# Attention over a context in four head pairs: maxima two blocks further ahead, a second buffer for the row sums, the outputs' scaling inside the last pair, and keys loaded early

## The reference

```python
ln = layer_norm(latents); xn = layer_norm(x)          # 512 and 8192 rows of 512
q = (ln @ Wq)                                         # 8 heads of 64, scaled by 64 ** -0.5
k_x, v_x = rope(xn @ Wk), xn @ Wv                     # rope turns halves of 32 within each head
k = concat([k_x, ln @ Wk]); v = concat([v_x, ln @ Wv])   # 8704 keys per head
out = softmax(q @ k.T) @ v                            # per head
x = x + out @ Wo
```

## Time and profile before

| | us |
|---|---|
| median of 3 runs (2338.95 to 2342.64) | 2342.53 |
| the profiled execution's own time | 2343.25 |
| its span | 2341.4 |
| context stage, first unit of maxima to last value product | 83.0 to 466.6 |
| attention, first scores to the next stage's first matmul | 485.3 to 1127.2 |
| TensorE busy in the span | 2171.3 |
| VectorE busy | 1659.6 |
| ScalarE busy | 1100.9 |
| GpSimd busy | 976.2 |

### The profile page before, as it was taken

The page is one execution under the profiler, slowest core; times in us unless marked ns, Lnnn a source line. Parts: engine busy times, 40 slices in busy tenths (PEclk is TensorE's granted clock), DMA queues, the critical chain, the costliest instruction groups (busy, mean ns, idle before and its releaser), DMA issues. The chain is left out here.

```text
span 2341.4 us, 38336 instructions
## 1 busy us (share of the span) xinstructions
PE 2171.3 (93%) x12632; PEld 1100.2 (47%) x12735; DVE 1659.6 (71%) x2398; ACT 1100.9 (47%) x1718; POOL 976.2 (42%) x651
## 2 busy tenths in 40 slices
PE   6899999979999899899699999999999999999858
PEld 2444444423223233233365664757565575757433
DVE  6677777569889889879575756666675756666672
ACT  4122222234444445456364655656464655656343
POOL 0243434469889699788220402122220302222040
PEclk9999999989999999999899999999999999999979
DMA  3345454343322323332323333342323333342330
GB/s 116 132 143 179 140 171 149 101 148 94 87 75 82 127 78 90 117 89 73 119 73 109 97 119 92 127 118 91 114 94 115 93 126 100 119 125 73 94 108 18
DMA packets 159717, 252.60 MB, mean 108 GB/s; under 512 B 11382, under 2 KB 63862, under 8 KB 159606
## 3 DMA queue, kind: packets, MB, share of 16 engines
q1 hardware_dynamic: 159606, 250.96, 33.7%
HBM read 212.00 MB, written 36.70 MB: 106 GB/s over the span
## 5 line engine op out<-in xcount | busy, mean ns | idle before, releaser
L817 POOL TENSOR_TENSOR h_lo<-h_lo,probs 128x896 f32<-128x896 f32 (+1 forms) x272 | 544.6, 2002 | 57.5 <-ACT probs L929 37.2
L63 PE MATMUL l_mm<-l_xt_hi,wt_hi 128*128 128x256 f16 (+3 forms) x1568 | 416.0, 277 | 5.2 <-DVE l_xt_lo L1259 2.8
L1218 POOL TENSOR_TENSOR l_rstd<-l_var_eps,neg_half 128x1 f32<-128x1 f32 x68 | 65.6, 965 | 844.9 <-DVE l_var_eps L1270 844.9
L65 PE MATMUL l_mm<-l_xt_hi,wt_lo 128*128 128x256 f16 (+3 forms) x1568 | 415.2, 276 | 1.4 <-issue 0.7
L64 PE MATMUL l_mm<-l_xt_lo,wt_hi 128*128 128x256 bf16 (+3 forms) x1560 | 412.8, 276 | 0.0
L929 ACT ACTIVATE probs<-sc 128x1024 f32<-128x1024 f32 x272 | 274.5, 1023 | 291.5 <-PE sc L977 239.0
L874 DVE TENSOR_TENSOR h_lo<-h_lo,probs 128x128 f32<-128x128 f32 (+1 forms) x272 | 295.6, 1087 | 24.4 <-ACT probs L929 23.5
L832 DVE TENSOR_REDUCE pmax<-mx 128x1024 f32 x204 | 249.0, 1220 | 41.8 <-PE mx L964 33.1
L988 PE MATMUL pv<-probs,vb 128*64 128x512 f32 x1088 | 268.4, 615 | 0.0
L976 PE MATMUL sc<-q_hi,ka 128*128 128x512 f16 x544 | 212.5, 391 | 13.2 <-DMA kh<-keys 5.9
L65 PE MATMUL l_tok<-wt_hi,h_lo 128*128 128x512 f16 x576 | 218.3, 379 | 1.7
(11 more groups left out here) (268 smaller groups left out, 3651.4 us busy)
## 6 DMA issues: line engine op xcount, KB each, us to landing
stage<-in_L_attn_Wf SPq DMA_DIRECT2D x64, 1024.0 KB, 5.2
keys<-wt_hi SPq DMA_DIRECT2D x136, 128.0 KB
ka<-keys SPq DMA_DIRECT2D x68, 256.0 KB, 3.3
vb<-values SPq DMA_DIRECT2D x68, 256.0 KB, 5.6
stage<-in_ctx SPq DMA_DIRECT2D x16, 1024.0 KB, 9.7
values<-wt_lo SPq DMA_DIRECT2D x16, 1024.0 KB
stage<-in_L_ffn_f SPq DMA_DIRECT2D x16, 1024.0 KB, 5.4
kh<-keys SPq DMA_DIRECT2D x68, 128.0 KB, 5.3
```

Source lines behind the costliest of these rows:

```text
L63: pe.matmul(out, lh, rh, start=first, stop=False, **kw)
L65: return pe.matmul(out, ll, rh, start=False, stop=last, **kw)
L817: g.tensor_tensor(sums[:, mine], sums[:, mine], probs[j][:, mine], ALU.add)\
```

## The change

- **Maxima two blocks further ahead.** While pair p works on block b, the maxima are those of the next pair's block b + 2 (max_block); in the last two blocks they are blocks 0 and 1 of the pair after next. For pair 1 these two come from the context stage, as four late units each in blocks 1 and 2, from a second set of km copies. Block 15's units of pair 0 also become late units, inside block 15. Odd pairs keep blocks 0 and 1 in two more columns of pmax, and the blocks are taken in another order (max_memory).
- **Pairs without a break.** pair_max and rows_of_maxima come before the last block or two of a pair, the first two score steps of the next pair inside its last block, row_sums behind the next pair's first block. There are two tiles sums.
- **Outputs.** ScalarE copies pv behind the next pair's first exponential and side in its second block, for each pair into its own place. The reciprocals of pairs 0 to 2 are taken in pair 3 behind blocks 1, 4 and 7; pair 3's reads side and pv directly.
- **Keys early.** ka and kh for blocks 0 and 1 of pair 0 are loaded in context block 15, in the place of res; the constant rows of kh are set at the program's start.

```diff
+MAX_COLS = KB + 2
+EARLIER_OUT = (1, 4, 7)
...
+        def earlier_units(b):
+            return TT * b + (2 * TT if not isinstance(b, int) or b >= 3 else TT if b == 2 else 0)
+        def late_pair(i, u):
+            b = 2 * i + u
+            if isinstance(b, int) and b in (1, 2):
+                return b - 1, 1
+            return (b, 0) if isinstance(b, int) and b == CTX_BLOCKS - 1 else None
...
@@ context_phase, SyncE, body
-                        sp.wait_ge(mx_ready, TT * b)
+                        sp.wait_ge(mx_ready, earlier_units(b))
...
+                    if late_pair(i, u) and late_pair(i, u)[1]:
+                        sp.wait_ge(mx_ready, earlier_units(b) + TT)
+                        sp.sem_inc(passed, 1)
+                        load_km(1 - u, 1 - u, 1)
                     for hl, done in enumerate((k_hi_done, k_lo_done)):
                         sp.wait_ge(done, 4 * b + 4)
...
+                    if not before_end(i, u, 1):
+                        for n in range(2):
+                            sp.wait_ge(stored[n], STORES * (HALF_BLOCKS - 1))
+                            k.load_k(sp, 0, n, n)
...
@@ context_phase, TensorE, body
                     values(i, u, 0)
+                    late_unit(0)
                     if more:
                         transposes(*nxt, 0)
                         transposes(*nxt, 1)
                     values(i, u, 1)
+                    late_unit(1)
...
@@ attention_phase
-        sums = rows(k.h_lo, 8, 4)
+        sums = [rows(k.h_lo, 8, 4), slots(k.wt_lo, 0, 1, F32, 2 * TOK)[:, 0]]
...
+        def max_block(p, b):
+            if isinstance(b, int) and b >= TURN:
+                return p + 2, b - TURN
+            return p + 1, b + 2
...
@@ VectorE
-                for n in range(2):
-                    v.memset(kh[n][HD:HD + 1], M_UNIT).then_inc(consts, 1)
...
+                            if b in EARLIER_OUT:
+                                n = EARLIER_OUT.index(b)
+                                dve.wait_ge(pv_copied, n + 1)
+                                dve.wait_ge(sums_copied, n + 1)
+                                out_scale(n, o_sum[:, n, :], o_raw[:, n, :])
+                            if b - 1 in EARLIER_OUT:
+                                out_low(EARLIER_OUT.index(b - 1))
...
+                        with dve.Fori(FIRST_PIECE + 1, TURN) as b:
+                            block_work(p, b, True)
+                    pair_max(p + 1)
+                    for b in range(TURN, KB):
+                        block_work(p, b, p > 0)
...
+                out_scale(PAIRS - 1, side[:], pv[:])
                 out_low(PAIRS - 1)
@@ ScalarE
+                    for b in range(2):
                         for j in range(SUB):
+                            exponential(p, b, j)
+                            if p and b == 0 and j == 0:
+                                out_copy(p - 1)
+                            if p and b == 1 and j == 1:
+                                sums_copy(p - 1)
...
+                    for j in range(SUB):
+                        exponential(p, KB - 1, j)
+                        if j == 1:
+                            row_maxima(p + 1)
@@ TensorE
                             elif not last:
-                                scores(p, i, u + 1, n) if u == 0 else scores(p, i + 1, 0, n)
+                                scores(p, b + 1, i, n)
+                            elif p + 1 < PAIRS:
+                                if n == 0:
+                                    pe.wait_ge(rows_done, 2 * (p + 2))
+                                scores(p + 1, 0, 0, n)
+                        if isinstance(i, int) and b == 0 and j == 0:
+                            if p:
+                                pe.wait_ge(pv_copied, p)
+                            t_.matmul(pv[:], zero[:], k.q_hi[:, 0, :], start=True, stop=False)
...
                 for p in range(PAIRS):
+                    block_steps(p, 0)
                     if p:
                         row_sums(p - 1)
-                        pe.wait_ge(out_copied, 2 * p)
...
+                    block_steps(p, KB - 2)
                     if p + 1 < PAIRS:
                         rows_of_maxima(p + 1)
+                    block_steps(p, KB - 1)
```

More of the change, by code:

```diff
@@ L40, with km_rows @@
     pass
-KM_ROWS = [(slice(HD * e + 32 * half, HD * e + 32 * half + 32), (slice(32 * e, 32 * e + 32), half))
-           for e in range(2) for half in range(2)]
+def km_rows(pair):
+    return [(slice(HD * e + 32 * half, HD * e + 32 * half + 32), (slice(HD * pair + 32 * e, HD * pair + 32 * e + 32), half))
+            for e in range(2) for half in range(2)]
 def slots(w, first, count, dtype, width):
@@ L360, in context_phase @@
         STORES = 16 * (2 * PAIRS + 1)
+        KM_IN = 16 * len(km_rows(0))
         def over_blocks(eng, body):
-            for u in range(2):
-                body(0, u)
-            with eng.Fori(1, HALF_BLOCKS - 2) as i:
+            for b in range(4):
+                body(b // 2, b % 2)
+            with eng.Fori(2, HALF_BLOCKS - 2) as i:
                 for u in range(2):
@@ L393, in load_tab, with load_km @@
                     sp.dma_start(tab[u][:], tab_v[2 * i + u]).then_inc(tab_in[u], 16)
+                def load_km(slot, u, pair):
+                    for rows_, (part, m) in km_rows(pair):
+                        sp.dma_start(km[slot][rows_, :], kt[u][part, 0, m, :]).then_inc(km_in[slot], 16)
                 def store_keys(i, u, hl, tile):
@@ L675, in body @@
                     values(i, u, 2)
+                    late_unit(2)
                     if more:
@@ L678, in body @@
                     values(i, u, 3)
+                    late_unit(3)
                 over_blocks(pe, body)
-                last = CTX_BLOCKS - 1
-                for j in range(TT):
-                    unit_max(TT + TT * last + j, 1, j, HALF_BLOCKS if j == 0 else None)
 def attention_phase(k):
@@ L720, in attention_phase @@
         side = pb("side", [P, TOK], F32)
-        k_loaded = [sem(f"a_k_loaded{n}") for n in range(2)]
         v_loaded = [sem(f"a_v_loaded{n}") for n in range(2)]
@@ L883, in _ @@
-                    with dve.Fori(0, KB - PIECES + 1 if p else KB) as b:
-                        block_work(b, False)
+                    if p == PAIRS - 1:
+                        for b in range(KB):
+                            if b == FIRST_PIECE + 1:
+                                dve.wait_ge(w_staged, 16 * STAGES * p)
+                            block_work(p, b, b > FIRST_PIECE)
+                            if b in EARLIER_OUT:
[5 more added lines that the diff above has]
+                                out_low(EARLIER_OUT.index(b - 1))
+                        weight_low(p, KB)
+                        continue
@@ L931, in _ @@
-                    with act.Fori(0, KB - PIECES if p else KB) as b:
-                        exponentials(b)
+                            exponential(p, b, j)
[3 more added lines that the diff above has]
+                                sums_copy(p - 1)
+                    if p == PAIRS - 1:
+                        for b in range(2, KB):
+                            if b == FIRST_PIECE:
+                                act.wait_ge(w_staged, 16 * STAGES * p)
+                            for j in range(SUB):
+                                exponential(p, b, j)
+                                if j == 1 and b - 1 in EARLIER_OUT:
+                                    out_high(EARLIER_OUT.index(b - 1))
+                            if b >= FIRST_PIECE:
+                                weight_high(p, b)
+                        continue
@@ L933, in _ @@
+                    with act.Fori(2, FIRST_PIECE if p else KB - 1) as b:
+                        for j in range(SUB):
+                            exponential(p, b, j)
                     if p:
                         act.wait_ge(w_staged, 16 * STAGES * p)
-                        with act.Fori(KB - PIECES, KB) as b:
-                            exponentials(b)
-                            n = b - (KB - PIECES)
-                            a.activation(hi_pieces[:, bass.ds(4 * XWO + PIECES * (p - 1) + n, 1), :],
-                                         staged_pieces[:, bass.ds(n, 1), :], ACT.Copy).then_inc(w_hi, 1)
@@ L940, in _ @@
-                    if p + 1 < PAIRS:
-                        row_maxima(p + 1)
-                    act.wait_ge(sums_ready, p + 1)
-                    if p >= 2:
-                        act.wait_ge(out_scaled, p - 1)
-                    a.activation(o_sum[p % 2], side[:], ACT.Copy).then_inc(out_copied, 1)
-                    a.activation(o_raw[p % 2], pv[:], ACT.Copy).then_inc(out_copied, 1)
+                        with act.Fori(FIRST_PIECE, KB - 1) as b:
+                            for j in range(SUB):
+                                exponential(p, b, j)
+                            weight_high(p, b)
```

307 lines of the change are left out of this document (168 added, 139 removed).

## The result

| | before | after |
|---|---|---|
| median of 20 runs each, us | 2343.19 (2338.41 to 2348.26) | 2337.49 (2332.49 to 2342.62) |
| ratio, 95% interval | | 0.9975 [0.9967, 0.9983] |
| span of the profiled execution | 2341.4 | 2333.8 |
| first scores of the attention | 485.27 | 502.88 |
| next stage's first matmul | 1127.23 | 1120.56 |

The change gains 5.7 us. The forecast was 2318 with a range to 2333, so the sign is right and the time falls outside the range: some 19 us of the gain are missing. They can be followed stretch by stretch.

The account below looks back on a forecast made before the run. TensorE bounds the context stage; in attention three engines run almost level, with the loss at the seams. 22.2 - 6.6 - 36.5 + 0.5 - 5.4 + 1.0 = -24.8 from 2343.25, less 0.7, gave 2318 us; range 2302 to 2333.

Parts of the forecast that it names:

- context stage, to the last store: Context stage: pair 1's late units, waits for copies and bank, lower clock and block 15's units make it 22.2 us later.
- the tail and the store: Behind the context stage: dropping the tail of four maxima gains hardly anything, early key loads may cost the store 0.5; counted 0.
- attention's start: Attention's opening: without two memsets and with keys loaded early, the chain of maxima alone decides; 6.6 us saved.
- seams (36.5): Three seams between attention pairs: 9.4, 14.7 and 10.9 us saved, plus 1.5 in pair 2's last blocks; together 36.5.
- keys behind weights: Two attention seams: block 2's keys queue right behind three weight loads, landing after they are needed; 1.0 us charged.
- reciprocals in pair 3: Last pair: three reciprocals on VectorE behind blocks 1, 4 and 7, mostly covered by four exponential buffers; 0.5 of 14.1 us charged.
- the end: From the last sums to the next stage: one reciprocal left instead of two in a row, 5.4 us saved.
- The seams' 3.7 us: Cost left at each seam: rows 1.48, sums 1.08, pv bank opening 0.2, pv copy 0.7, switching 0.2; 3.7 us.
- Keys wait at the seams: Rival: scores wait for keys at both seams as in the attention's opening, 10.7 us more than charged, 2329; chance 0.13.
- the reciprocals show: Rival: VectorE cannot catch up in pair 3, so the reciprocals cost 13.6 us more, 2332; chance 0.12.
- Slower than before: Rival: stalls leave TensorE at half clock over context blocks 1 and 2, 43 us more, 2362; chance 0.03.
- the seams stay: Rival: the next pair's scores still meet an unfinished row of maxima, so the 36.5 us remain, 2355; chance 0.03.

Follow-up runs that it names:

- own tiles: Changed kernel, with pair 1's context-stage km copies given two tiles of their own and loaded right behind pair 0's in blocks 0 and 1: 2319.17 us, ratio 0.9895.
- late keys: Changed kernel, with pair 0's first keys loaded at the attention's start again, ahead of the values, not in context block 15: 2335.15 us, ratio 0.9969.

## Why the prediction was wrong, step by step

| step of the prediction | forecast, us | measured, us |
|---|---|---|
| context stage, to the last store | +22.2 | +22.3 |
| the tail and the store | 0 | +1.6 (+3.2 for the early loads, -1.6 for the tail) |
| attention's start | -6.6 | -6.2 |
| seams (36.5), without the three steps below | -36.5 | about -34.5 |
| keys behind weights | +1.0 | +8.8 in the trace, 7.0 in the runs |
| reciprocals in pair 3 | +0.5 | +5.7 in the trace, 3.9 in the runs |
| the end | -5.4 | -4.3 (-5.5, and a wait 1.2 longer) |

The row of the seams is the rest: from the first scores to the next stage the attention went from 641.96 to 617.68 us, 24.3 less; with 8.8 and 5.7 added and the end's 4.3 taken off, 34.5 remain. The slow scaling costs 3.7 within them (1.64 and 2.02), so that without it the seams would have given 1.7 more than forecast. The forecast for the whole attention was 40.4.

- **The context stage** was right in its sum by luck. The waits for the copies are 12.9 us and not 9.4, there is no wait for the bank where I had 4.2, the eight units take 3.9 and not 2.6, those of block 15 1.3 and not 1.0, and the stage happened to begin 0.8 sooner. Only the clock is as charged: from the unit that waited to the next it is 6.79 and 6.17 us, and in the run with own tiles 4.00 (4.22 less a wait of 0.22), so the clock cost 2.8 and 2.2. The run with own tiles takes back 18.3 us by the medians and 16.1 in the trace, where copies, bank and clock stood at 18.6.
- **"I charge 1.0 us in two seams" is the step that failed most.** It failed twice. My own arithmetic had keys at 17 us and their need at 15.5, which is 3.0 for two seams, and I charged 1.0 without a reason. Measured from the old pair's end (816.60), they were needed at 16.4 and landed at 18.4 in pair 2; in pair 3 it was 13.0 and 14.9. The waits are 3.8. And I left out what the wait does to the clock, though I had charged just that in the context stage: what follows the two waits, 5.0 of the 8.8, is more than the waits. The run with weights spread out removes both. The Trainium skill, page "DMA: Bandwidth & Descriptors", section "Queues, rings and completion order", has each DMA engine take the descriptors of a queue in the order of the ring. The trace agrees: the keys were asked for 0.4 us behind the issue of the third weight load, that load landed 9.8 us after its issue at 822.15, near 832.0, the keys at 835.0.
- **"I charge 0.5 of the 14.1."** VectorE hides two reciprocals of three, as I argued, and not the one behind block 7. By then ScalarE and VectorE also split weights, and no idle time of VectorE is left. I took the four buffers for the whole cover. The timeline shows a shorter one: ScalarE's out_high stands behind the second exponential of the next block and holds the other two until VectorE's product is done, at 1047.1, where the buffers were free by 1043.1. Without it the next exponentials (block 9's first, due near 1045.9 at a pace of 3.72) would have waited only for VectorE's first sum of block 8, which ended near 1047.8; so I estimate that 2 of the 3.97 us come from out_high's place in the queue. No run moves it. Moved to blocks 3 and 5, 3.9 us come back, 4.4 in the trace, and without the waits for keys two reciprocals show by 1.5 us each. The bounds (0 and 14.1) held it; my pick near the lower end did not.
- **The seams' 3.7 us** lacked VectorE's part. I moved pair_max from a gap into a stretch where VectorE has no time to spare, and counted only TensorE's matmuls. 0.17 us in the old trace became 1.85, and twice held the bank. My own had shown this factor for another operation. The run with the scaling on ScalarE gives 3.6 in the trace and 2.7 in the medians.
- **The start** came out at the size forecast, but not for the reason that I gave. "With keys loaded before the stage ends it alone decides": the chain of maxima decides also with keys loaded late, in a good order. The early keys lengthen the time from the values store's issue to the new stage from 4.9 to 8.1 us, 3.2, for which I had charged at most 0.5, inside a count of 0. The tail of maxima, which I had bring hardly anything, had been worth 1.6: the kernel before needed 6.5 where late keys without the tail need 4.9.
- **The rivals.** "Keys wait at the seams" (10.7 more) and "the reciprocals show" (13.6 more) both held in part, 6 to 8 and 3 to 5 us. I gave each a chance of its own and a time of its own, but never the case that both come in at a third or more of their price, beside one unnamed loss. Nothing excludes that: they lie in different places. From 2318 that case is 2327 by the runs' prices (6.0 and 3.4 more than charged) and 2331 by the trace's (7.8 and 5.2); with the 1.6 of tail and store and the scaling's 2.7 to 3.7 it is 2332 to 2336. The result is 2337.5, so the range ended where it should have gone on. "Slower than before" and "the seams stay" are excluded: the clock is back after each stall, and no row of maxima is waited for.

Two of the signs that the prediction names for being wrong came: a wait on keys at block 2 of a pair, and ScalarE waiting for VectorE in pair 3.

Left open: what a later out_high would give; how often a short gap is followed by the lower clock; why the sums at the end wait 1.2 us longer; and why the keys' loss weighs more in the trace (8.8) than what the runs give back (7.0). For the reciprocals (5.7 and 3.9) the wait that stays, 1.35, is most of the answer.

## What to carry to other kernels

Work moved out of a gap must be priced in its new place: a tiny VectorE operation that took 0.17 us alone took 1.85 beside GpSimd, and small copies that landed in 1.9 us kept TensorE waiting for 6.5 once they stood behind stores. Where three engines run level, a stall can cost itself and the clock behind it: waits of about 2 us for keys came out at 5.3 and 3.5; add up the moderate cases as well as each rival alone. When a slow operation is to hide behind buffers, look for what else waits for it in order: here a copy in ScalarE's queue used up the cover. Before loading something earlier, try the order of the loads that are there: two loads moved behind the keys brought the first scores 4.5 us sooner (2.7 by the medians), nearly all that the early load was to give.

## What was not expected of the hardware

- A tensor_scalar of 128 x 8 elements on VectorE takes 0.17 us in the gap of the kernel before and 1.81 to 1.85 us beside GpSimd's sums over 128 x 896 (L891 at 640.93, 798.95 and 962.88). The tensor_reduce right ahead of it, 128 x 136 to 128 x 8, takes 0.28 in both. The Trainium skill, page "SBUF — State Buffer", section "SBUF: two separate sides", describes one port pair that VectorE in some modes and GpSimd take for a whole instruction. The trace agrees: six sums of GpSimd fill 631.93 to 644.90, 2.16 us each, so that the fifth ends near 642.7, and the scaling ends at 642.78. No run takes GpSimd's sums away, so this cause is argued and not shown. The same scaling on ScalarE takes 0.21 in the attention's opening.
- The granted clock fell behind waits of TensorE of only about 2 us: 0.72 over 12 us behind one of 1.99. Behind the gap of about 1.8 us at seam 1 to 2 it fell in three executions of seven (0.77, 0.89 and 0.89 over 15 us).
- The stage behind a 1 MB store began 4.9 us after its issue with no loads near it in the queue, and 8.1 us after it where four loads of 0.75 MB in all stood ahead.
